# Cross-attention on one core: the running maximum reads ScalarE's SBUF copy of a score chunk instead of the score bank

## What is computed

```python
def _cross_attention(q_in, kv_in, wq, bq, wk, bk, wv, bv, wo, bo, bias_k, bias_v):
    qh = (q_in @ wq + bq).reshape(b, q_len, H, K)
    kh = (kv_in @ wk + bk).reshape(b, t, H, K)
    vh = (kv_in @ wv + bv).reshape(b, t, H, K)
    kh = jnp.concatenate([kh, jnp.broadcast_to(bias_k, (b, 1, H, K))], axis=1)
    vh = jnp.concatenate([vh, jnp.broadcast_to(bias_v, (b, 1, H, K))], axis=1)
    logits = jnp.einsum('bqhk,bthk->bhqt', qh, kh) / scale
    weights = jax.nn.softmax(logits, axis=-1)
    ctx = jnp.einsum('bhqt,bthk->bqhk', weights, vh).reshape(b, q_len, H * K)
    return ctx @ wo + bo

x = x + _cross_attention(_layer_norm(x, ...), ctx_2048, ...)   # layer 1
x = x + _cross_attention(_layer_norm(x, ...), ctx_2048, ...)   # layer 2
return x + gelu(_layer_norm(x, ...) @ w_fc1 + b_fc1) @ w_fc2 + b_fc2
```

## Time and profile before

| | us |
|---|---|
| median of 3 runs | 1225.71 (1225.41 to 1227.16) |
| the profiled execution | 1225.35 |
| its span in the profile | 1223.6 |
| TensorE busy | 1202.5 (98% of the span) |
| VectorE busy | 847.8 (69%) |
| ScalarE busy | 764.7 (62%) |
| GpSimd busy | 870.1 (71%) |

### The profile page before, as it was taken

How to read it: one execution, slowest core, us unless ns; L and a number is a source line. 1 busy time by engine, 2 the same in 40 slices (tenths; PEclk the granted TensorE clock), 3 DMA queues, 4 the chain that set the end, 5 groups by cost and what they waited for, 6 DMA issues and landing times.

```text
span 1223.6 us, 26581 instructions
## 1 busy us (share of the span) xinstructions
PE 1202.5 (98%) x7736; PEld 1109.9 (91%) x7736; DVE 847.8 (69%) x1392; ACT 764.7 (62%) x1501; POOL 870.1 (71%) x744
## 2 busy tenths in 40 slices
PE   7999999999999999999999999999999999999998
PEld 6869999999999999998986999999999999999998
DVE  6956767676767676776675667676767777767754
ACT  4745666666666665676584656565656565667765
POOL 4837787878787877676552768686868686867762
PEclk9999999999999999999999999999999999999999
DMA  5401222222222222133320122222222222222331
GB/s 173 136 18 51 57 77 55 76 55 76 55 76 55 76 55 76 43 72 97 107 78 18 39 57 65 67 64 66 65 66 67 64 70 62 69 51 71 77 92 42
DMA packets 147721, 83.60 MB, mean 68 GB/s; under 512 B 121117, under 2 KB 122541, under 8 KB 147673
## 3 DMA queue, kind: packets, MB, share of 16 engines
q1 hardware_dynamic: 147128, 82.27, 25.7%
q10 hardware_dynamic: 544, 0.75, 0.2%
HBM read 68.56 MB, written 0.53 MB: 56 GB/s over the span
## 4 chain that ended last, share of the span: by engine, by line
PE 93%; DVE 2%; DMA 2%; issue 1%; ACT 1%; POOL 1%; SPq 0%; DVEq 0%; POOLq 0%; ACTq 0%
PE psum L781 39%; PE psum L798 13%; PE psum L799 13%; PE psum L800 13%; PE psum L747 5%; PE psum L843 5%; PE psum L768 2%; DMA w_raw<-weights 1%; PE psum L697 1%; PE psum L822 0%; DMA dk_first<-dk_rows 0%; PE psum L793 0%; PE psum L788 0%; POOL ctx L551 0%; ACT slots L1079 0%
## 5 line engine op out<-in xcount | busy, mean ns | idle before, releaser
L609 POOL TENSOR_TENSOR pt<-slots,pt 125x512 fp32r<-125x512 f32 (+3 forms) x384 | 450.8, 1181 | 171.7 <-ACT slots L1079 162.9
L781 PE MATMUL psum<-qs,ctx 128*125 128x384 f32 (+1 forms) x2304 | 538.5, 370 | 3.0 <-ACT slots L1105 2.3
L781 PEld LDWEIGHTS psum<-qs,ctx 128*125 128x125 f32 x2304 | 394.4, 186 | 50.8 <-ACT slots L1105 10.1
L798 PE MATMUL psum<-ctx,pt 125*128 125x258 f32 (+1 forms) x1344 | 380.8, 283 | 0.6 <-POOL pt L609 0.5
L799 PE MATMUL psum<-ctx,pt 125*128 125x256 f32 (+1 forms) x1344 | 379.4, 282 | 0.0
L800 PE MATMUL psum<-ctx,pt 125*128 125x258 f32 (+1 forms) x1344 | 379.0, 282 | 0.0
L1078 ACT ACTIVATE pt<-slots 125x512 fp32r<-125x512 f32 (+3 forms) x384 | 221.2, 576 | 248.1 <-DVE slots L1364 241.2
L1376 DVE TENSOR_TENSOR t_max<-psum,t_max 125x512 f32<-125x512 f32 (+1 forms) x320 | 198.8, 621 | 184.4 <-PE psum L781 183.3
L1105 ACT ACTIVATE slots<-psum 125x512 f32<-125x512 f32 (+1 forms) x384 | 205.6, 536 | 112.6 <-DVE t_max L1376 102.2
L798 PEld LDWEIGHTS psum<-ctx,pt 125*128 125x128 f32 (+1 forms) x1344 | 253.6, 189 | 11.1 <-issue 1.3
L799 PEld LDWEIGHTS psum<-ctx,pt 125*128 125x128 f32 (+1 forms) x1344 | 254.1, 189 | 6.7
(11 more groups left out here) (108 smaller groups left out, 965.7 us busy)
## 6 DMA issues: line engine op xcount, KB each, us to landing
nat_stage<-ctx_nat SPq DMA_DIRECT2D x60, 375.0 KB
tr_stage<-ctx_tr SPq DMA_DIRECT2D x60, 375.0 KB, 3.1
w_raw<-weights SPq DMA_DIRECT2D x70, 256.0 KB, 2.7
qt<-turn SPq DMA_DIRECT2D x256, 32.0 KB, 2.0
qt<-turn SPq DMA_DIRECT2D x224, 24.0 KB, 1.9
dk_rest<-dk_rows SPq DMA_DIRECT2D x2, 768.0 KB, 5.7
w_raw<-weights ACTq DMA_DIRECT2D x2, 256.0 KB, 4.5
dk_first<-dk_rows SPq DMA_DIRECT2D x2, 256.0 KB, 4.6
```

The costliest lines, as they stand in the source:

```text
L609: nc.gpsimd.tensor_tensor(split_weights(h, LO, c), logits(h, c), as_f32(split_weights(h, HI, c)), ALU.subtract).then_inc(pt_lo, 1)
L781: last = mm(scores(h, k), ctx_tr_chunk(half, a, c), qs[h][:, m, half, 0:R], start=(half, a, m) == terms[0], stop=(half, a, m) == terms[-1])
L798: mm(out_bank[:, 0:D + 2], hi, ctx_nat_hi(c), start=(c == 0), stop=False, skip_group_check=True)
```

## The change

The copy now waits for the matmul in all steps. The maximum waits for the copy of the same chunk instead of the matmul, and reads `slots` instead of the bank; with that wait the extra one of c = 1 is contained in it. Nothing is added, removed or moved in any engine's order, and no buffer changes. With lines taken out, the copy is L1102 and the maximum L1372 in the kernel after.

```diff
@@ ScalarE, batch_steps @@
                         if not tail:
                             if first and k == NCT:
                                 act.wait_ge(lb_written, l * 16 + 16)
-                            if c == 0:
-                                act.wait_ge(s_mm, INIT + l * LAYER_STEPS + b * STEPS + (k + 1))
-                            else:
-                                act.wait_ge(max_done, INIT + group * (NCT - 1) + c)
+                            act.wait_ge(s_mm, INIT + l * LAYER_STEPS + b * STEPS + (k + 1))
                             go(slot(h, c), scores(h, k), ACT.Copy).then_inc(copied, 1)
@@ VectorE @@
                 def chunk_max(b, k, h, c):
 
                     done = (l * GROUPS + b * 2 + h) * (NCT - 1)
-                    dve.wait_ge(s_mm, INIT + l * LAYER_STEPS + b * STEPS + (k + 1))
+                    dve.wait_ge(copied, INIT + l * LAYER_STEPS + b * STEPS + (k + 1))
                     if c == 1:
-                        dve.wait_ge(copied, INIT + l * LAYER_STEPS + b * STEPS + k)
                         before = slot(h, 0)
                     else:
                         dve.wait_ge(max_done, INIT + done + (c - 1))
                         before = t_max[h][0:CT]
-                    V.tensor_tensor(t_max[h][0:CT], scores(h, k), before, ALU.max).then_inc(max_done, 1)
+                    V.tensor_tensor(t_max[h][0:CT], slot(h, c), before, ALU.max).then_inc(max_done, 1)
```

## The result

| | us |
|---|---|
| before, median | 1225.62 |
| after, median of 4 runs | 1712.65 (1711.31 to 1713.70) |
| ratio | 1.397, 95% interval 1.395 to 1.399 |
| the profiled execution's span, before and after | 1223.6 and 1709.5 |

A forecast was written before the change was run, and what follows sets the result against it. TensorE, busy 98%, was taken to bound the kernel before; the ring with the block would replace it. Full batches 440, first batches 20 and clock 28 us sum to 488 on 1225: 1713, said as 1715 us, range 1585 to 1830.

The forecast's parts named there:

- TensorE bound before: Whole kernel before: TensorE busy for 98% of the span, VectorE 69%, ScalarE 62%, GpSimd 71%.
- the prize at most 10 us: Weight loads for the scores (L781) waiting for the bank's copy: 10.1 us in 24 waits, an upper bound.
- The ring: Each subtracting step: subtraction, two exponentials, copy, maximum, next subtraction become one chain, 2.65 or 2.75 us against 2.52.
- The block at the port: Maximum with two SBUF inputs waits until GpSimd's subtraction ends; steps become 3.16 and 3.65 us; chance of ring with block 0.70.
- The rival without the block: Ring only, steps of 2.65 and 2.75 us, batch 76.5 us, total 1450 us; chance 0.14.
- the hop: Way from ScalarE's copy back to VectorE's maximum in each step, taken as 0.05 us.
- A batch: A full batch of 24 steps: 92.0 us against 60.6, +31.4 each, times 14: +440 us.
- Steps: Steps with the block: 3.16 us when subtracting 384 columns, 3.65 when subtracting 512; ten of each kind a batch.
- The first batch: First batch of each layer: ten steps of the second kind plus two casts, +12 us, twice +24, less 4: +20.
- the 4 us put down as gain: Steps ahead of the first batch's subtracting ones: earlier free bank gives back up to 10 us, 4 taken.
- The clock: TensorE's clock falls after idling some 3.6 us at group ends: 1 us twice a batch, 28 us over 14.
- Signs named ahead: Profile after: maxima 1.2 and 1.45 us, batches about 92 us, TensorE busy near 70%, clock under 1.00 in some loop slices.

The follow-up runs named there:

- hybrid: Kernel before, but in each layer's first 14 steps the copy waits for the matmul and the maximum reads the SBUF copy behind it; 1226.0 us, ratio 1.000.
- copy_first: Kernel after with ScalarE's copy of the chunk moved ahead of the step's exponentials and scalings; 1349.9 us, 1.101 to before.
- ring_bank: Kernel after, but the maximum reads the score bank again, still behind the copy, and TensorE waits for maximum and copy; 1507.1 us, 1.229 to before.
- warm_less: Kernel after with added matmuls of no use, 2 in steps with c of 2 or more and 14 at a group's end; 1702.3 us, 1.389 to before.
- exp_copy_exp: Kernel after with ScalarE's copy placed between the two exponentials of a step; 1434.3 us, 1.171 to before.
- scale_copy_bank: Kernel after with the maximum reading the bank, TensorE waiting for copy and maximum, ScalarE's order scalings, copy, exponentials; 1235.6 us, 1.008 to before.

## Why the prediction was right

Point by point, by its own steps.

*TensorE bound before, the prize at most 10 us.* Right, and smaller still: the earlier release of the bank, tried where nothing speaks against it (hybrid), gives nothing that shows (1226.0 us, a ratio of 0.999 to 1.001).

*The ring.* Right in kind and size. It appears as two waits that face each other, 553 us and 763 us, and goes away when only ScalarE's order is changed (copy_first: 363 us less).

*The block at the port.* Right. GpSimd ends at 424.04 and 485.82, the maxima 0.55 and 0.41 us later, as the pair of the earlier trace rows had it (0.52 us for 480 columns). Taking the second SBUF input away takes 206 us away, and starting the maximum first turns the block around. This is what the Trainium skill's page "SBUF — State Buffer", section "Who interferes with whom", states for a VectorE instruction with two SBUF inputs beside a GpSimd instruction that reads SBUF; the runs here agree, with 1.12 and 1.39 us where GpSimd comes first against 0.71 and 0.64 where the maximum mostly does. The same section says of an instruction with at most one SBUF input that it stays free of this outside VectorE's 2-port modes; the prediction left that condition out. No run shows the mode of an instruction, but VectorE's transposed casts, with one SBUF input, are blocked in these kernels (last section). The rival without the block was put at 1450 us; ring_bank, which keeps the ring and has no block, took 1507, so the block is worth 206 us and not 263. The 0.07 us that the hop lacked count only without the block: with it the maximum waits for GpSimd anyway.

*A batch.* Steps 3.16 and 3.65 us predicted, 3.17 and 3.65 measured; 92.0 and 92.5 us a batch. By the starts of one instruction in all of them the seven full batches of a layer take 92.6 us on average, +32.0 each, 448 us over 14. With the clock's 9 to 10 us taken out (they lie in these batches) 438 to 439 are left, and 440 were predicted. Single steps are off by up to 0.3 us either way (in warm_less step 0 took 2.83 us for 3.1 and step 10 3.44 for 3.16), and these errors nearly cancel.

*The first batch: mis-sized.* The prediction put +12 us a layer less 4 in all, +20. The part from step 12 to the next batch's step 0 took 25.45 us before and 42.88 after, by the transposes that stand at its two ends. Before:

```profile
80.14 0.73 DVE L1384 STREAM_TRANSPOSE psum<-t_max 128x512 f32<-128x512 f32 x1
...
105.59 0.58 DVE L1384 STREAM_TRANSPOSE psum<-t_max 128x384 f32<-128x384 f32 x1
```

After, with the first maximum ahead of it:

```profile
66.23 0.80 DVE L1372 TENSOR_TENSOR t_max<-slots 125x512 f32<-125x512 f32 x1 [1.36 <-ACT slots L1102]
...
80.86 0.73 DVE L1380 STREAM_TRANSPOSE psum<-t_max 128x512 f32<-128x512 f32 x1
...
123.74 0.58 DVE L1380 STREAM_TRANSPOSE psum<-t_max 128x384 f32<-128x384 f32 x1
```

These are +17.4 us a layer, +35 in all. The error was to price the ten steps of the kernel before at 2.52 us each, 25.2 in all. They took 20.6 us (the subtractions from 84.44 to 105.00 us), as the first of them have no weighted sum yet. The same ten in the kernel after took 37.5 us (85.67 to 123.14), and 37.4 were predicted. And the 4 us put down as gain ahead of them did not come. The eleven maxima of the first half run from 66.23 to 80.13 us in place of 64.05 to 79.41, so 1.46 us closer, but they start later (some 1 us with all that stands ahead of the scores, the rest behind the copy), and the half ends at 80.86 against 80.14.

*The clock: mis-sized.* The mechanism is there. TensorE idles 4.19 us at this group's end and 3.9 on average (3.6 were estimated), the granted clock is 0.50, that is 1.2 GHz, in the 2 us that follow, and back at 1.00 four us later:

```profile
261.69 0.37 PE L788 MATMUL psum<-ident,mx_part 128*16 128x128 f32 x1 [4.19 <-DVE mx_part L1382]
```

Stretches (from and to, length, busy us of PE, PEld, DVE, ACT and POOL, granted clock, DMA share, GB/s):

```profile
262.00:264.00 2.00, 2.00 (x8) 2.00 (x8) 1.14 (x2) 0.73 (x2) 1.81 (x3) 0.50 0.10 16
264.00:266.00 2.00, 2.00 (x12) 1.83 (x11) 1.20 (x2) 0.63 (x2) 1.34 (x2) 0.74 0.00 0
266.00:268.00 2.00, 2.00 (x16) 2.00 (x16) 2.00 (x3) 0.00 (x0) 0.30 (x1) 1.00 0.00 0
```

But its price is 10 us by warm_less and not 28: some 0.3 us at each of 28 group ends, where 1 us was predicted. VectorE's wait for the second transpose, in which it has to show, is 9.1 us in all, and 3.0 in warm_less. The rest of the slower work lies beside the ring. The two mis-sized terms point in opposite directions, 15 us too little and 18 too much, and this is why the total is 2 us from the measured one. That closeness is luck; the ring, the block and the length of a batch are not. By steps the prediction is good to about 4% of the difference, not to 0.5%. Batches and first batches give 483 of the 487 us; the other 4 lie outside them. In the two traces, whose spans differ by 486 us, 0.7 us lie ahead of the first transpose (L1380), 0.5 between the layers and 1.7 behind them.

*Signs named ahead.* The maxima at 1.2 and 1.45 us were 1.12 and 1.39, batches at 92 were 92.5, the clock under 1.00 was 0.914 over the span. TensorE's busy share of 70% was 79%: the same work takes longer at the lower clock, 1354 us in place of 1202.

*What stays open.* Of exp_copy_exp's and ring_bank's distance from the expected times only the named parts are shown. Ring_bank and the two kernels that build on it differ from their partners in one thing more than the source: TensorE waits for the maximum too. What that wait costs was not tried by itself. The last 10 us of scale_copy_bank over before were not taken apart; the later exponentials and the maximum behind the copy are both still in it.

## What to carry to other kernels

Before one engine is made to wait for another, follow that one's queue backwards to the first thing that waits for you: if the awaited instruction stands behind work that depends on an earlier instruction of your own queue in the same step, two queues become one chain, and its length (not the busy shares, here 69% and 62%) is the new time of a step. The length can be read from the timeline of before, hop by hop. If the wait has to stay, the order on the other engine is what opens the ring (363 us here), but look at what is pushed back by it: here the scalings, for 31 us. And an operand that moves from PSUM to SBUF can become VectorE's second SBUF input, and what this costs is set by what GpSimd is doing at that moment: 0.43 us a maximum of 512 columns and 0.85 of 384 here.

## What the runs showed of the hardware

- The end of the blocked instruction is a better number to predict than its length. In the kernel after 174 maxima of 384 columns and 160 of 512 start while GpSimd is at work. The first end 0.41 or 0.42 us behind GpSimd's end and the second 0.55 to 0.58, whenever they had begun, though they last from 1.02 to 1.48 and from 0.69 to 1.56 us. The subtraction of 480 columns in the earlier trace rows ended 0.52 us behind.
- One of VectorE's two casts from SBUF to SBUF is blocked as well, the other is not. The transposed one (L1252, 128x750) takes 0.54 us beside an idle GpSimd and up to 2.12 when it starts behind a GpSimd instruction. The natural one (L1246, 125x768) takes 0.93 to 0.96 us either way. One of each in the kernel before, VectorE's line first and then GpSimd's; the blocked one ends 0.42 us behind GpSimd's L544:

```profile
333.17 0.95 DVE L1246 CAST ctx<-nat_stage 125x768 fp32r<-125x768 f32 x1 [0.39 <-DMA nat_stage<-ctx_nat]
...
335.10 2.07 DVE L1252 CAST ctx<-tr_stage 128x750 fp32r<-128x750 f32 x1
...
332.49 2.56 POOL L609 TENSOR_TENSOR pt<-slots,pt 125x512 fp32r<-125x512 f32 x2
335.00 1.75 POOL L544 TENSOR_TENSOR ctx<-nat_stage,ctx 125x768 fp32r<-125x768 f32 x1
```

- In the kernel after, GpSimd is idle at 56 of the 60 transposed casts, and their mean fell to 554 ns from 1098 before. So each adds 0.54 us to the ring and not 1.1.
- A lowered clock can cost little. In the kernel after TensorE was busy for 152 us more than before with the same matmuls, and bringing its clock from 0.914 to 0.977 over the span gave back only 10 us of 1713. The likely reason is that most of the slow matmuls ran while VectorE and ScalarE worked through their chain.
